# One maximum over six blocks of scores for a pair of heads, a join of the second tile's maxima, and the weights' scales written column by column

## The reference, cut to what matters

```python
q = layernorm(x) @ Wq.T;  k, v = split(ctx @ Wkv.T)          # 16 heads of 32
scores = where(causal, (q @ k.T) / sqrt(32), lowest)         # 256 x 256 for a head
x = x + tanh(g_x) * (softmax(scores) @ v) @ Wout.T
h = layernorm(x)
# qlinear: the input is divided by its row's largest |value| / 448 and rounded to FP8, the weight too
t = silu(qlinear(h, w_gate)) * qlinear(h, w_up)              # 1408 wide
x = x + tanh(g_f) * qlinear(t, w_down)
```

## Time and profile before

| | |
|---|---|
| median of 3 runs | 742.82 us (742.79 to 743.15) |
| the profiled execution | 744.06 us |
| its span, first to last instruction | 742.3 us |
| mean granted clock of PE | 0.965 |
| busy PE / DVE / ACT / POOL | 663.5 / 664.0 / 552.3 / 551.3 us |
| chain that ended last, by engine | PE 69%, DVE 12%, ACT 8%, DMA 4%, POOL 2% |
| the two reduces L1690 and L1691 | 53.5 and 87.3 us busy, 128 of each |

### The profile page before, as it was taken

How to read it: one execution, slowest core, us unless ns; L and a number is a source line. 1 busy time by engine, 2 the same in 40 slices (tenths; PEclk the granted TensorE clock), 3 DMA queues, 4 the chain that set the end, 5 groups by cost and what they waited for, 6 DMA issues and landing times.

```text
span 742.3 us, 15885 instructions
## 1 busy us (share of the span) xinstructions
PE 663.5 (89%) x6130; PEld 420.9 (57%) x6130; DVE 664.0 (89%) x1193; ACT 552.3 (74%) x987; POOL 551.3 (74%) x606
## 2 busy tenths in 40 slices
PE   2566889899999999999999999999999999888672
PEld 2445666566666666666565656565666666443220
DVE  6997866989999999899999989898989899998983
ACT  4978779796878787878788787879697959384430
POOL 6577897877878787878879787878787876575341
PEclk9858899999999999999999999999999999999996
DMA  8889776768575666685757565765748565130321
GB/s 288 205 193 165 158 161 106 151 147 155 127 133 115 144 122 135 98 173 92 169 89 157 105 153 112 142 129 129 132 122 137 134 100 133 24 100 16 79 67 48
DMA packets 151208, 95.52 MB, mean 129 GB/s; under 512 B 115326, under 2 KB 121854, under 8 KB 151134
## 3 DMA queue, kind: packets, MB, share of 16 engines
q1 hardware_dynamic: 148974, 92.68, 59.9%
q0 software_dynamic: 576, 1.45, 0.6%
q10 hardware_dynamic: 1584, 0.39, 0.2%
HBM read 31.59 MB, written 9.83 MB: 56 GB/s over the span
## 4 chain that ended last, share of the span: by engine, by line
PE 69%; DVE 12%; ACT 8%; issue 4%; DMA 4%; POOL 2%; SPq 0%; ACTq 0%; POOLq 0%; DVEq 0%
PE pair L730 37%; PE pair L957 6%; PE pair L962 5%; PE pair L932 3%; PE pair L987 3%; PE pair L983 3%; PE pair L988 3%; PE pair L931 2%; PE pair L891 2%; DVE mx L1691 2%; PE pair L893 2%; PE pair L892 2%; DMA PT<-in_L_xattn_Wq_dram 1%; DMA Q<-mT 1%; DVE rsum L1695 1%
## 5 line engine op out<-in xcount | busy, mean ns | idle before, releaser
L607 POOL TENSOR_TENSOR room<-room,up_scale 128x512 f32<-128x512 f32 (+1 forms) x96 | 121.9, 1277 | 43.6 <-ACT room L1363 43.2
L591 POOL TENSOR_SCALAR_AFFINE_SELECT PT<-PT 128x512 f32<-128x512 f32 x128 | 88.0, 700 | 41.6 <-ACT PT L1338 40.7
L1338 ACT ACTIVATE PT<-pair 128x768 f32<-128x768 f32 x128 | 99.8, 810 | 12.8 <-PE pair L962 6.4
L1363 ACT ACTIVATE room<-room,sx 128x512 f32<-128x512 f32 (+1 forms) x96 | 64.9, 679 | 47.3 <-DVE room L1762 47.2
L730 PE MATMUL pair<-WdT,room 128*128 128x512 bf16 x352 | 85.3, 393 | 14.8 <-DMA room<-room 9.8
L730 PE MATMUL pair<-WgT,room 128*128 128x512 bf16 (+1 forms) x384 | 91.3, 361 | 7.0 <-DMA room<-room 3.8
L730 PE MATMUL pair<-WuT,room 128*128 128x512 bf16 (+1 forms) x384 | 91.3, 362 | 1.9 <-DVE room L1762 1.7
L730 PE MATMUL pair<-xT,WqTh 128*128 128x256 bf16 x512 | 88.6, 275 | 1.7 <-ACT exact L1150 1.7
L1691 DVE TENSOR_REDUCE mx<-pair 128x2 f32<-128x512 f32 x128 | 87.3, 682 | 0.0
L1368 ACT ACTIVATE room<-room 128x512 bf16<-128x512 f32 (+1 forms) x96 | 54.7, 586 | 39.6 <-DVE room L1779 38.7
L730 PE MATMUL pair<-xT,WqTl 128*128 128x256 bf16 x256 | 70.5, 275 | 0.0
(11 more groups left out here) (137 smaller groups left out, 1902.6 us busy)
## 6 DMA issues: line engine op xcount, KB each, us to landing
xin<-in_x_dram SPq DMA_DIRECT2D x16, 512.0 KB
K<-kh SPq DMA_DIRECT2D x32, 256.0 KB
Q<-qh SPq DMA_DIRECT2D x32, 256.0 KB
x<-in_x_dram SPq DMA_DIRECT2D x16, 512.0 KB, 4.5
out_dram<-x SPq DMA_DIRECT2D x16, 512.0 KB, 3.1
K<-kl SPq DMA_DIRECT2D x16, 256.0 KB
Q<-kl SPq DMA_DIRECT2D x16, 256.0 KB
room<-in_L_ffn_w_down_dram SPq DMA_DIRECT2D x4, 704.0 KB, 7.5
```

Source lines behind the costliest of these rows:

```text
L591: pool.affine_select(out=view, in_=view, compare_op=ALU.is_ge, fill=0.0, base=0, pattern=[[0, 2], [0, 2], [1, P]], channel_multiplier=-1). ...
L607: pool.tensor_tensor(g, g, up_scale[:, chunk(n)[1]], ALU.mult).then_inc(slw_done, 1)
L1338: act.activation(head_columns(ring(b, c), 0, 384), head_columns(shifted_pair[c][:, :], 0, 384), ACT.Exp, scale=SCALE).then_inc(exp_done, 1)
L1363: act.activation(g, g, ACT.Silu, scale=sx[:, chunk(n)[0]:chunk(n)[0] + 1]).then_inc(silu_done, 1)
```

## The change

1. `maxima(b, c)` is one reduce over blocks 0, 1 and 2 of both heads (128 x 768 elements read), into three columns for each head. `mx` is wider by one column.
2. A new DVE instruction for each batch, `second_maxima(b)`, placed right behind `maxima(b, 7)`, takes the larger of the columns 1 and 2 for all 16 heads. It waits for the last reduce and raises a new semaphore, for which POOL's `max_parts` now waits. `max_parts` reads two of the three columns through a strided view.
3. `pair_scales` makes its scales by one instruction for each column: 26 in place of 8.
4. Waits are left out where another wait already implies them, on all five engines, and a few are put elsewhere or in another order (`k_ones` and the second masks are now waited for in `scores`). Among those left out: ACT's waits for its own copies in `attention_weights_exact`, `keys_exact` and `queries_exact` (for b of 1 and more the latter has no wait left), the wait for `v_done` in `scores(b, 0)` for b of 1 and more, the wait for `cut_done` in `weighted(b, 0)` from b = 3. Waits that DVE needs before writing over `gs` (`t_done` in gates 3 and 4) stay.
5. The loops are written out for the first and last batches, with a loop for k of 1 to 8. The order of the steps on each of the five engines is the same as before, but for the 16 `second_maxima`. No DMA is added, removed or moved.

```diff
-        mx = sb("mx", [P, NH, TT])
+        mx = sb("mx", [P, NH, TT + 1])
...
             def maxima(b, c):
                 dve.wait_ge(s_made, 8 * b + c + 1)
...
-                dve.tensor_reduce(mx[:, heads, 0], head_columns(w, 0, P), AX.X, ALU.max)
-                dve.tensor_reduce(mx[:, heads, 1], head_columns(w, P, 3 * P), AX.X, ALU.max).then_inc(max_done, 1)
+                dve.tensor_reduce(mx[:, heads, :], head_columns(w, 0, 3 * P).rearrange("p h (r s) -> p h r s", s=P), AX.X,
+                                  ALU.max).then_inc(max_done, 1)
+
+            def second_maxima(b):
+                dve.wait_ge(max_done, 8 * b + 8)
+                dve.tensor_tensor(mx[:, :, 1], mx[:, :, 1], mx[:, :, 2], ALU.max).then_inc(max_joined, 1)
...
             def max_parts(b):
-                pool.wait_ge(max_done, 8 * b + 8)
-                m = mx[:, :, :].rearrange("p h t -> p (h t)")
-                chained(pool.tensor_copy(m_parts[:, 0, :], m))
-                chained(pool.tensor_tensor(m_rest[:, :], m, m_parts[:, 0, :], ALU.subtract))
+                pool.wait_ge(max_joined, b + 1)
+                m = mx[:, :, 0:TT]
+                first = m_parts[:, 0, :].rearrange("p (h t) -> p h t", t=TT)
+                chained(pool.tensor_copy(first, m))
+                chained(pool.tensor_tensor(m_rest[:, :].rearrange("p (h t) -> p h t", t=TT), m, first, ALU.subtract))
...
-                dve.tensor_scalar(wmult[:, j, i:end], winv[:, j, i:end], FP8_MAX, None, ALU.mult).then_inc(w_scales, 1)
+                for m in range(i, end):
+                    last = dve.tensor_scalar(wmult[:, j, m:m + 1], winv[:, j, m:m + 1], FP8_MAX, None, ALU.mult)
+                last.then_inc(w_scales, 1)
...
             def queries_exact(b, j):
-                act.wait_ge(kl_done, 2 * b + j + 1)
-                act.wait_ge(qh_done, 2 * b + j + 1)
+                if b == 0:
+                    act.wait_ge(kl_done, j + 1)
                 copy(exact[:, j, :], q_bank[j]).then_inc(q_exact, 1)
...
             def attention_weights_exact(n):
-                if n == 0:
-                    act.wait_ge(aw_high, 1)
...
-                if n == 2:
-                    act.wait_ge(aw_high, 3)
...
             def scores(b, c):
                 if c == 0:
                     pe.wait_ge(m_cleared[b % 2], 16 * (b // 2) + 16)
                     pe.wait_ge(q_stacked, 48 * b + 48)
-                    pe.wait_ge(v_done, 2 * b + 1)
                 if c == 0 and b == 0:
+                    pe.wait_ge(v_done, 1)
...
             def weighted(b, g):
-
-                if g == 0:
+                if g == 0 and b <= 2:
                     pe.wait_ge(cut_done, 8 * b + 2)
+                if g == 0 and b == 0:
+                    pe.wait_ge(exp_done, 5)
+                if g == 0 and b >= 2:
                     pe.wait_ge(exp_done, 8 * b + 5)
```

More of the change, by code:

```diff
@@ L1986, in _ @@
[L1986 to L2000 removed]
+                lifted_x(k - 1, 1)
@@ new lines, in _ @@
+            gate(8, 0)
+            floored_t(7, 1)
+            maxima(10, 3)
+            residual(9, 0)
+            maxima(10, 4)
+            maxima(10, 5)
+            maxima(10, 6)
+            maxima(10, 7)
+            second_maxima(10)
+            gate(8, 1)
+            lifted_t(7, 1)
+            up(8, 0)
+            gate(8, 2)
+            gate(8, 3)
+            rounded_t(7, 1)
+            up(8, 1)
+            gate(8, 4)
+            up(8, 2)
+            largest_t(8, 0)
+            gate(8, 5)
@@ new lines, in _ @@
+            maxima(11, 5)
+            maxima(11, 6)
+            maxima(11, 7)
+            second_maxima(11)
+            gate(9, 1)
+            lifted_t(8, 1)
+            up(9, 0)
+            gate(9, 2)
+            gate(9, 3)
+            rounded_t(8, 1)
+            up(9, 1)
+            gate(9, 4)
+            up(9, 2)
+            largest_t(9, 0)
+            gate(9, 5)
+            largest_t_inverted(9, 0)
+            floored_t(9, 0)
+            lifted_t(9, 0)
+            rounded_t(9, 0)
@@ new lines, in _ @@
+            rounded_x(12, 1)
+            gate(12, 0)
+            floored_t(11, 1)
+            maxima(14, 3)
+            residual(13, 0)
+            maxima(14, 4)
+            maxima(14, 5)
+            maxima(14, 6)
+            maxima(14, 7)
+            second_maxima(14)
+            gate(12, 1)
+            lifted_t(11, 1)
+            up(12, 0)
+            gate(12, 2)
+            gate(12, 3)
+            rounded_t(11, 1)
+            up(12, 1)
+            gate(12, 4)
+            up(12, 2)
@@ new lines, in _ @@
+            maxima(15, 3)
+            residual(14, 0)
+            maxima(15, 4)
+            maxima(15, 5)
+            maxima(15, 6)
+            maxima(15, 7)
+            second_maxima(15)
+            gate(13, 1)
+            lifted_t(12, 1)
+            up(13, 0)
+            gate(13, 2)
+            gate(13, 3)
+            rounded_t(12, 1)
+            up(13, 1)
+            gate(13, 4)
+            up(13, 2)
+            largest_t(13, 0)
+            gate(13, 5)
+            largest_t_inverted(13, 0)
```

2871 lines of the change are left out of this document (2096 added, 775 removed).

## The result

Five runs of each kernel on one chip: before 743.11 us (742.79 to 744.03), after **747.21 us** (746.08 to 748.92), a ratio of 1.0058 with a 95% interval of 1.0044 to 1.0073. The change makes the kernel slower by 0.6%. The prediction said 741.7 us, with a range that ended at 743.7. Both profiled executions lie near these medians: 744.06 us with a span of 742.3 before, 747.21 us with a span of 745.4 after.

A forecast was written before the change was run, and what follows sets the result against it. PE's stream was taken to bound eleven of the sixteen batches, so only start and end could move the time. Terms for reduces, join and ScalarE's copies summed to -1.15 us, from 742.82 to 741.7 us, range 739.8 to 743.7.

The forecast's parts named there:

- sum of -1.15 us: Whole kernel: reduces -0.52 and -0.26, join +0.31 and +0.2, ScalarE's copies -0.57 and -0.31; everything else at 0.
- Only these ends can move the time: Start up to about 158 us and end after batch 15's reduces set the time; PE's stream hides savings between.
- I cost them at nothing: Waits left out, except ScalarE's on its own copies: nearly all already satisfied, so 0 us.
- The rival: Join stopped by GpSimd in every batch, PE waiting 0.34 us in each of 12: +4, about 746 us; chance 0.07.
- spare 0.36 us: Between the maxima's DMA landing and PE's first product needing it: a delay from 0.36 us a batch makes PE wait.
- The reduces: One merged reduce taking 0.85 to 0.87 us saves 0.065 a pair: -0.52 at the end, -0.26 at the start.
- The join: New small DVE instruction behind each batch's last reduce: +0.25 and +0.06 at the end, +0.2 in batch 2, elsewhere nothing.
- ScalarE's copies: Start-up, without waits for its own copies: -0.57 for exact queries of batches 1 to 3, -0.31 for attention's weights.
- gains taken up: Rival: DMAs of weights or stacked queries set the start, only the end remains: -0.2, 742.6 us; chance 0.15.
- The scales: Scales by column between 9 and 115 us: 18 more DVE instructions, covered, so 0; bounds -1.0 and +1.0.
- Slower by over 0.2%: Outcome of over 1.5 us slower: the join stopping every batch and a little of a slower reduce; chance 0.08.

The follow-up runs named there:

- a1: The kernel before with 64 unused bytes behind the maxima tile, so all later tiles lie as in the changed kernel; no instruction changed: 747.08 us, ratio 1.0044.
- a2: The changed kernel with the three-column maxima allocated last, so every other tile lies where the kernel before has it: 746.29 us, ratio 1.0041.
- a4: The changed kernel with tiles at their old addresses and 38 satisfied waits at the front of PE's program: 743.63 us, ratio 1.0001.
- e2: The changed kernel with every tile of a DMA at a multiple of 256 bytes, its PE program as it is: 742.41 us, ratio 0.9994.
- d3: The changed kernel with every tile of a DMA at a multiple of 256 bytes and 38 satisfied waits at PE's front: 741.33 us, ratio 0.9976.
- b5: The kernel before without ScalarE's waits for its own copies (queries and attention's weights), no tile moved: 743.48 us, ratio 1.0009.
- b1: The kernel before with 128 unused bytes right in front of `room`, so only `room` moves: 745.48 us, ratio 1.0029.
- b2: The kernel before with 64 unused bytes right in front of `room`: 745.65 us in a single run.
- b3: The kernel before with 192 unused bytes right in front of `room`: 745.97 us in a single run.
- c1: The kernel before with only the weights' scales made column by column, 26 instructions for 8: 742.94 us, ratio 0.9999.
- c2: The kernel before with every tile a DMA reads or writes at a multiple of 256 bytes, instructions unchanged: 741.49 us, ratio 0.9979.
- a3: The changed kernel with 38 satisfied waits added at the front of PE's program, tiles not moved back: 746.28 us, ratio 1.0041.

## Why the prediction was wrong

**The first step that failed is a term put at nothing without a word.** The sum of -1.15 us treats the reduce and the join as a matter of instructions. The diff's first line, one more column in `mx`, has no term in it, and what lies behind that tile in memory is not looked at. Measured: 0.44% (a1), some 3 us. With it fell "Only these ends can move the time": the steady stretch became 1.0 us longer.

**The second is "I cost them at nothing",** said of the waits left out. It is right of waiting and wrong of the program's length. That 38 instructions less shift the moments at which PE's program is fetched, and that such a fetch can hold up a transpose, was on no list. Measured: 0.41% (a2, the whole change but for the places; a4 without the fetch at that moment has 0.01%), and about 1.1 us with aligned tiles (e2 less d3).

**The rival came nearer than the forecast, for a wrong reason.** The prediction named PE's spare 0.36 us before `Q<-mT` as the point from which things go wrong, and about 746 us as the price. PE did wait there, in more batches. But what used up the spare time was not the join, which takes 0.18 us in every steady batch and ends 9.62 us behind the batch's first reduce, exactly where the last reduce used to end. It was the transfer; that 747.21 us came out near the rival's 746 is luck. The margin itself was misread: 0.36 us is batch 10's 4.36 less the 4.00 that batch 15's DMA took, while batch 10's own DMA landed 3.75 us after its issue, which leaves 0.61. A margin of this size should have been held against everything that touches that DMA, not just against what stands ahead of its issue.

**The reduces** are right: 0.87 us from one to the next at the end (3.47 us for four, foretold 0.85 to 0.87), mean 0.953 (0.95). In batch 15 the stretch from the first reduce's start to the last one's end fell from 9.62 to 9.10 us, 0.52 less, which is the term. With the join it is 0.31 less, and 0.30 less at the issue of the maxima's DMA; the sum had 0.52 - 0.31 = 0.21.

**The join** was put at 0.25 us at the end and is 0.21 there, with its gap. In batch 2 it was foretold to begin no sooner than GpSimd's end; it began at once and took 0.51 us, until GpSimd was done, which for the time is the same. The rule of the Trainium skill's page "SBUF — State Buffer", section "Who interferes with whom", that an operation with two SBUF inputs can be held by GpSimd, is borne out by these two rows.

**ScalarE's copies** do start closer, 0.47 us for 0.69, but the gain of 0.88 did not arrive (b5). Against the kernel before, the changed one is 0.73 us ahead at batch 1's scores, 0.42 at batch 2's and 0.08 at batch 3's (172.61 for 172.69). That is the rival "gains taken up". A single profile says little here: in before, a1, b1, b2 and b3, whose instructions are the same up to there (their tiles are not at the same places), batch 3's scores begin at 172.69, 173.34, 171.68, 172.41 and 170.88 us. The start differs between them by more than every term that I had for it.

**The scales** at nothing: right (c1). **The sum** of -1.15 us, freed of the two causes, was still too good: a4 measured 1.0001 (0.9992 to 1.0010), which leaves out -0.15%. What is missing is above all ScalarE's 0.88 us, which b5 shows not to arrive.

**Chances.** "Slower by over 0.2%" had 0.08. All of it was given to mechanisms in the diff's instructions; with so little to spare behind a transfer, more should have been left for what the instructions don't show.

## What to carry to other kernels

Before changing the size of any tile in on-chip memory, list which tiles stand behind it and whether those that DMAs transpose stay at multiples of 256 bytes; put odd-sized tiles last, and align the rest as c2 does, which by itself gave 0.2%. When an edit takes instructions out of an engine's program or adds some, see whether one of its fetches now falls into a transfer that an engine stands waiting for; a few satisfied waits at the front of the program shift it. When a transfer lands late, compare its last semaphore update with the others before blaming the engine that waits. And when two versions differ by less than 1%, run the old one with nothing but the new layout before explaining the difference by the new work.

## What the runs showed that was not expected

- A transpose's packets of 256 bytes take 17.9 ns if `room` begins at a multiple of 256 bytes and 21.1 to 22.2 ns at 64, 128 or 192 past one. SP's issue shows it too: 1334 to 1336 ns at the least in every run with the first, 1357 or 1358 in every run with the second.
- A fetch of 16,384 bytes of PE's program, 1.0 to 1.3 us long, that falls into the last part of a transpose can hold back one of its sixteen semaphore updates by 1.5 to 1.9 us, and with it the engine that waits. A fetch of 8,192 bytes of another engine does it too. In the changed kernel such a fetch runs from 698.16 to 698.47, and the store of an output tile beside it has its fifteenth update at 698.70 and its sixteenth at 699.60; the kernel before has no fetch there, and the same two updates come 0.01 us apart.
- Two waits in a row on an already reached count take one instruction: 38 waits added 19 to PE's records (a2 to a4).
- The granted clock after PE's stop before the maxima's products was low in some executions and not in others. Where it was, between 655 and 662 us, the time from batch 15's scores to the end was 107.2 to 107.9 us (a1, a3, b3, b5); with the clock full there, b1 and b2, as slow in their packets as a1, took 105.5 and 106.1. That is of the size by which runs of one kernel scatter; what decides it is open.
